# Expert bias on TensorE, D times x on ScalarE, gated output weights on VectorE, and a new order of work in an adaLN + Mamba-2 + MoE block

## What is computed

```python
mod = (silu(c) @ wmod)                      # sa, ca, ga, sb, cb, gb of each sequence
h = layernorm(x) * (1 + ca) + sa
x = x + ga * mamba2(h)                      # |ga| at least 0.25
h = layernorm(x) * (1 + cb) + sb
x = x + gb * moe(h)                         # |gb| at least 0.25
```

## Time and profile before

| | |
|---|---|
| median of 3 runs | 949.03 us (946.83 to 950.27) |
| the profiled execution | 949.21 us, of which the span from first to last instruction is 947.4 us |
| PE matmul busy | 701.8 us (74%) |
| DVE busy | 631.7 us (67%) |
| POOL busy | 596.0 us (63%) |
| ACT busy | 419.7 us (44%) |
| DMA | 93.05 MB, mean 98 GB/s |
| granted TensorE clock, mean | 0.871 |

### The profile page before, as it was taken

One profiled execution on the slowest core, in us unless ns is written; L12 is line 12 of the kernel. 1 busy time (PEld: TensorE's weight loads), 2 busy tenths in 40 slices (PEclk: granted clock), 3 DMA queues, 4 the chain that ended last, 5 costly groups with the idle time before them and its releaser, 6 DMA issues. The chain is left out here.

```text
span 947.4 us, 13162 instructions
## 1 busy us (share of the span) xinstructions
PE 701.8 (74%) x3642; PEld 549.3 (58%) x3642; DVE 631.7 (67%) x1654; ACT 419.7 (44%) x821; POOL 596.0 (63%) x437
## 2 busy tenths in 40 slices
PE   1578698698788799789978989788946737576570
PEld 1236466466566677667856767577835526454450
DVE  2445958978988997997999999988734413223230
ACT  2364663673774575467556654553323112111210
POOL 1035436567675878787878887797786654444444
PEclk9988987998899997989999999888979668777876
DMA  5000001111223554455356346435566685555642
GB/s 168 0 0 1 1 23 29 45 51 52 81 89 105 129 127 100 113 117 144 74 120 143 102 89 150 118 88 102 146 172 137 162 201 129 128 106 130 125 110 22
DMA packets 80456, 93.05 MB, mean 98 GB/s; under 512 B 7344, under 2 KB 66880, under 8 KB 80384
## 3 DMA queue, kind: packets, MB, share of 16 engines
q1 hardware_dynamic: 53712, 65.58, 24.7%
q0 software_dynamic: 26672, 26.62, 16.0%
HBM read 59.24 MB, written 32.93 MB: 97 GB/s over the span
## 5 line engine op out<-in xcount | busy, mean ns | idle before, releaser
L428 POOL DMA_INDIRECT out<-ro,xs x142 | 226.5, 1595 | 152.8 <-DVE ro L1026 79.3
L415 POOL DMA_INDIRECT rows<-payload,pos x128 | 134.8, 1053 | 47.0 <-issue 33.3
L824 DVE SCALAR_TENSOR_TENSOR xbc<-T,table,xbc 128x1022 f32<-128x1022 f32 (+2 forms) x96 | 122.7, 1278 | 31.5 <-ACT xbc L577 26.7
L1180 PE MATMUL T<-h,win 128*128 128x512 f32 x128 | 82.3, 777 | 56.4 <-DVE xbc L824 45.2
L1026 DVE SCALAR_TENSOR_TENSOR ro<-osum,xs 128x128 f32<-128x128 f32 x142 | 78.4, 594 | 60.0 <-DMA out<-ro,xs 59.8
L1343 PE MATMUL FX<-wt,hid 128*128 128x128 f32 x568 | 95.2, 322 | 31.2 <-DVE hid L1009 12.4
L1343 PEld LDWEIGHTS FX<-wt,hid 128*128 128x128 f32 x568 | 90.2, 232 | 43.3 <-DVE hid L1009 24.1
L626 ACT ACTIVATE xt<-FX 128x256 f32<-128x256 f32 x71 | 27.1, 382 | 188.3 <-PE FX L1323 176.8
L1333 PE MATMUL FG<-xt,wt 128*128 128x256 f32 x284 | 91.5, 453 | 6.3 <-issue 3.6
L619 ACT ACTIVATE sg<-FG,wt 128x256 f32<-128x256 f32 x142 | 59.2, 470 | 79.5 <-PE FG L1333 72.8
L1017 DVE TENSOR_TENSOR osum<-FX,wt 128x256 f32<-128x256 f32 x71 | 29.9, 421 | 85.1 <-PE FX L1343 76.2
(11 more groups left out here) (173 smaller groups left out, 1489.0 us busy)
## 6 DMA issues: line engine op xcount, KB each, us to landing
wt<-in_wt SPq DMA_DIRECT2D x71, 450.0 KB
xs<-rows SPq DMA_DIRECT2D x71, 258.0 KB
x<-in_x SPq DMA_DIRECT2D x8, 512.0 KB, 3.9
out<-x SPq DMA_DIRECT2D x8, 512.0 KB
rows<-pad SPq DMA_DIRECT2D x9, 258.0 KB, 5.0
out<-ro,xs POOLq DMA_INDIRECT x142
rows<-payload,pos POOLq DMA_INDIRECT x128
gate_a<-gates SPq DMA_DIRECT2D x8, 128.0 KB
```

The lines of the kernel that those rows point to most:

```text
L415: pool.indirect_dma_start(d["rows"], bass.IndirectOffsetOnAxis(ap=pos[:, k, n:n + 1], axis=0), payload[:, n, :], None).then_inc(scattered, 16)
L428: pool.indirect_dma_start(d["out"], bass.IndirectOffsetOnAxis(ap=xs[:, t % XSR, c, PAY - 1:PAY].bitcast(U32), axis=0), ro[:, t % 2, c, :], ...
L824: last = nc.vector.scalar_tensor_tensor(out=xbc[:, t, :, k:L], in0=T[:, :, 0:L - k], scalar=w, in1=xbc[:, t, :, k:L], op0=ALU.mult, op1=AL ...
L1180: last = nc.tensor.matmul(T[:, k, :], win[:, o:o + P], h[:, k * L:(k + 1) * L], start=True, stop=True)
```

## The change

- `expert_sum` and `osum` are gone. PE adds b3 by one more matmul for each 128 rows (a row of ones times the row of b3), two for each tile. `expert_out` reads FX in PSUM directly, into one of three `ro` buffers instead of two; PE's next use of FX waits for `ro_ready` instead of `o_taken`, and a weight buffer is free after `expert_down`.
- The landing of output adds is counted on two semaphores, for even and odd tiles; `add_out(t)` still waits for tiles t - 2 and t - 1.
- `weight_by_d` moves from POOL to ACT, as four activations with a scale for each chunk (16 for a pair). `gated_wo` moves from POOL to DVE.
- The expert of a tile is worked out from its row number (regions of 18432 rows in place of 8448), so three DVE instructions of `list_tiles` fall away.
- The order on all engines is new. On SP, weights now follow the rows of a same or later tile, `store_x1(i)` stands ahead of rows 8i - 17 and weights 8i - 18 and 8i - 17, and weights 8i - 23 stand behind rows 8i - 22. On POOL, `weight_by_decay(i, 1)` opens the step, and the dt and decay weights of chunk 2 stand behind two scatters and `add_out` of tiles 8i - 27 and 8i - 26. On ACT, `decay_exp` 0 to 7 stand together with no SiLU between them, and `expert_silu(8i - 18)` comes behind them; `softplus_exp` and `second_tanh` follow each other with no SiLU between.

The diff, cut (the order of DVE, and most of that of ACT and PE, is left out):

```diff
-REGION = NTOK + TR
+FIRST = TR
+REGION = 18432
-DUMP = E * REGION
+DUMP = E * REGION + FIRST
-WR, XSR = 4, 5
+WR, XSR, RR = 4, 5, 3
...
-        ro = sb("ro", [P, 2, 2, D])
+        ro = sb("ro", [P, RR, 2, D])
...
+        def landed(eng, t):
+            if t >= 0:
+                eng.wait_ge(added[t % 2], 32 * (t // 2 + 1))
...
             def load_weights(t):
                 sp_.wait_ge(seq_ready, pair_of_tile(t) + 1)
-                wait(sp_, o_taken, t - WR + 1)
+                wait(sp_, o_psum, t - WR + 1)
...
-                wait(sp_, added, 32 * (t - XSR + 1))
+                landed(sp_, t - XSR)
...
             for i in range(-3, 12):
-                if is_tile(PT * i - 23):
-                    load_rows(PT * i - 23)
-                if is_tile(PT * i - 22):
-                    load_rows(PT * i - 22)
                 if is_tile(PT * i - 21):
                     load_rows(PT * i - 21)
+                if is_pair(i):
+                    load_gates(i)
+                if is_tile(PT * i - 22):
+                    load_weights(PT * i - 22)
+                if is_tile(PT * i - 21):
                     load_weights(PT * i - 21)
...
                 if is_tile(PT * i - 18):
-                    load_weights(PT * i - 18)
                     load_rows(PT * i - 18)
+                if is_pair(i):
+                    store_x1(i)
                 if is_tile(PT * i - 17):
                     load_rows(PT * i - 17)
+                if is_tile(PT * i - 18):
+                    load_weights(PT * i - 18)
+                if is_tile(PT * i - 17):
                     load_weights(PT * i - 17)
-                if is_pair(i + 1):
-                    load_gates(i + 1)
                 if is_tile(PT * i - 16):
+                    load_rows(PT * i - 16)
                     load_weights(PT * i - 16)
-                    load_rows(PT * i - 16)
-                if is_pair(i):
-                    store_x1(i)
+                if is_pair(i + 3):
+                    reload_x(i + 3)
+                if is_tile(PT * i - 15):
+                    load_rows(PT * i - 15)
+                if is_tile(PT * i - 14):
+                    load_rows(PT * i - 14)
                 if is_tile(PT * i - 15):
                     load_weights(PT * i - 15)
-                if is_pair(i + 3):
-                    reload_x(i + 3)
-                if is_tile(PT * i - 14):
-                    load_weights(PT * i - 14)
...
             def add_out(t):
-                pool.wait_ge(ro_ready, t + 1)
-                pool.wait_ge(added, 32 * t) if t > 0 else pool.wait_ge(dump_set, 32)
+                if t == 0:
+                    pool.wait_ge(dump_set, 32)
+                landed(pool, t - 2)
+                landed(pool, t - 1)
                 pool.wait_ge(x1_stored, 16 * (pair_of_tile(t) + 1))
                 pool.wait_ge(xs_in[t % XSR], 16 * (t // XSR + 1))
+                pool.wait_ge(ro_ready, t + 1)
...
             for i in range(-2, 13):
                 if is_pair(i):
-                    weight_by_d(i, 1)
                     weight_by_decay(i, 1)
                 if is_pair(i - 2):
                     scatter(i - 2, 6)
-                if is_pair(i):
-                    weight_by_dt(i, 2)
                 if is_tile(PT * i - 27):
                     add_out(PT * i - 27)
                 if is_pair(i - 2):
                     scatter(i - 2, 7)
-                if is_pair(i):
-                    weight_by_decay(i, 2)
                 if is_tile(PT * i - 26):
                     add_out(PT * i - 26)
                 if is_pair(i):
-                    weight_by_d(i, 2)
-                    weight_by_dt(i, 3)
+                    weight_by_dt(i, 2)
+                    weight_by_decay(i, 2)
...
+            def weight_by_d(p, c):
+                act.wait_ge(tok_ready, C * p + c + 1)
+                wait(act, y_ready, C * p + c - 1)
+                for hh in range(NH):
+                    e = slice(hh * HD, (hh + 1) * HD)
+                    last = nc.scalar.activation(xskip[:, c % 2, :, e], tok[:, c, :, e], ACT.Copy, scale=d_row[:, hh:hh + 1])
+                last.then_inc(xskip_ready, 1)
...
+            def gated_wo(p):
+                vec.wait_ge(gate_a_in[p % 2], 16 * (p // 2 + 1))
+                wait(vec, out_psum, p)
+                nc.vector.tensor_tensor(out=wo[:, :, :, :], in0=woutn[:, :, :].unsqueeze(1).to_broadcast([P, 2, 2, D]),
+                                        in1=gate_a[:, p % 2, :, :].unsqueeze(2).to_broadcast([P, 2, 2, D]),
+                                        op=ALU.mult).then_inc(wo_ready, 1)
...
-                link(nc.vector.tensor_tensor(out=mine[:, 0:n, :], in0=mine[:, 0:n, :],
-                                             in1=experts.unsqueeze(1).to_broadcast([P, n, E]), op=ALU.mult))
-                link(nc.vector.tensor_reduce(out=tile_sum[:, 0:n], in_=mine[:, 0:n, :], axis=AX.X, op=ALU.add))
-                link(nc.vector.tensor_tensor(out=seq_e[:, span], in0=seq_e[:, span], in1=tile_sum[:, 0:n], op=ALU.add))
...
-                nc.vector.tensor_copy(tile_e[:, span], seq_e[:, span])
+                nc.vector.tensor_scalar(tile_e[:, span], seq_row[:, span], 1.0 / REGION, E - 0.6, ALU.mult, ALU.min)
...
-            def expert_sum(t):
+            def expert_out(t):
                 vec.wait_ge(o_psum, t + 1)
-                wait(vec, ro_ready, t)
-                nc.vector.tensor_tensor(out=osum[:, :, :], in0=FX[:, TR:2 * TR].rearrange("p (c m) -> p c m", c=2),
-                                        in1=wt[:, t % WR, B3:].unsqueeze(1).to_broadcast([P, 2, D]),
-                                        op=ALU.add).then_inc(o_taken, 1)
-
-            def expert_out(t):
-                vec.wait_ge(o_taken, t + 1)
-                rows_in = xs[:, t % XSR, :, :]
-                wait(vec, added, 32 * (t - 1))
+                landed(vec, t - RR)
                 for c in range(2):
-                    last = nc.vector.scalar_tensor_tensor(out=ro[:, t % 2, c, :], in0=osum[:, c, :], scalar=rows_in[:, c, 2 * D:2 * D + 1],
-                                                          in1=rows_in[:, c, D:2 * D], op0=ALU.mult, op1=ALU.mult)
+                    last = nc.vector.scalar_tensor_tensor(out=ro[:, t % RR, c, :], in0=FX[:, TR + c * D:TR + (c + 1) * D],
+                                                          scalar=xs[:, t % XSR, c, 2 * D:2 * D + 1], in1=xs[:, t % XSR, c, D:2 * D],
+                                                          op0=ALU.mult, op1=ALU.mult)
                 last.then_inc(ro_ready, 1)
...
                 for c in range(2):
+                    nc.tensor.matmul(FX[:, TR + c * D:TR + (c + 1) * D], ones_r[0:1, :].bitcast(F32), wt[0:1, t % WR, B3:B3 + D],
+                                     start=True, stop=False)
                     for f in range(FT):
                         last = nc.tensor.matmul(FX[:, TR + c * D:TR + (c + 1) * D], hid[:, t % 2, f, c * P:(c + 1) * P],
-                                                wt[:, t % WR, DOWN + f * D:DOWN + (f + 1) * D], start=(f == 0), stop=(f == FT - 1))
+                                                wt[:, t % WR, DOWN + f * D:DOWN + (f + 1) * D], start=False, stop=(f == FT - 1))
                 last.then_inc(o_psum, 1)
-                back["FX"] = (o_taken, t + 1)
+                back["FX"] = (ro_ready, t + 1)
```

More of the change, by code:

```diff
@@ L378, in weight_by_dt @@
                                         op=ALU.mult).then_inc(xdt_ready, 1)
-            def weight_by_d(p, c):
-                wait(pool, tok_ready, C * p + c + 1)
-                wait(pool, y_ready, C * p + c - 1)
-                nc.gpsimd.tensor_tensor(out=xskip[:, c % 2, :, :], in0=tok[:, c, :, 0:DI],
-                                        in1=d_row.unsqueeze(1).to_broadcast([P, 2, DI]), op=ALU.mult).then_inc(xskip_ready, 1)
             def weight_by_decay(p, c):
@@ L454, in _ @@
                 if is_pair(i):
-                    gated_wo(i)
-                    weight_by_d(i, 3)
+                    weight_by_dt(i, 3)
+                if is_tile(PT * i - 24):
+                    add_out(PT * i - 24)
+                if is_pair(i + 1):
+                    masked_da(i + 1, 0)
+                    masked_da(i + 1, 1)
                 if is_pair(i - 1):
                     scatter(i - 1, 0)
-                if is_tile(PT * i - 24):
-                    add_out(PT * i - 24)
-                if is_pair(i - 1):
                     scatter(i - 1, 1)
@@ L467, in _ @@
                 if is_pair(i + 1):
[L468 to L469 removed]
+                    masked_da(i + 1, 2)
+                if is_pair(i - 1):
+                    scatter(i - 1, 3)
                 if is_tile(PT * i - 22):
@@ L654, in _ @@
                     second_tanh(i - 1)
-                if is_tile(PT * i - 24):
-                    expert_silu(PT * i - 24)
+                if is_tile(PT * i - 22):
+                    expert_input(PT * i - 22)
+                if is_pair(i):
```

(59 more changed lines are left out.)

306 lines of the change are left out of this document (121 added, 185 removed).

## The result

The changed kernel takes 962.15 us (median of 4 runs, 956.55 to 964.64) beside 947.93 for the kernel before (4 runs): ratio 1.0138, with an interval of 1.0102 to 1.0175. It is slower by 1.4%; 923 us and faster were forecast. The profiled execution took 956.55 us (span 954.7).

A forecast was written before the change was run, and what follows sets the result against it. VectorE was taken to bound the four full steps (90% busy), TensorE close behind, with order bounding the head and something serial the tail. 949.2 - 17 (steps) - 3 (head) - 3 (last pair) - 3 (tail) = 923 us; range 906 to 938.

The forecast's parts named there:

- The steps: Four steps running scan, projection and experts together: PE 316 us busy plus 16 idle, 332 us, 17 less; ends 324 and 364.
- VectorE no longer bounds: Four steps: DVE falls from 315 to about 270 us, 77%, with 32 us of it from `ro` read from PSUM.
- the list of wrong signs: Included blocked time turning up at L845, L889 or the new `gated_wo`, leaving DVE near 85% in the steps.
- PE's waits down to a third: Sign of being right: PE's waits for L824 (taps) and for FX fall to a third.
- D on ScalarE: D products on ACT: 16 activations of 128 elements a pair, 6.4 us a pair; bounds 4 and 8.
- The bias: PE in the four steps: 60 more matmuls, priced like today's by their columns, add 15 us; ends 0 and 17.6.
- rival 2: TensorE takes over at once: bias dear, steps 350 us and gain nothing, the rest gains 9, 940 us; chance 0.13.
- The head: Fewer table loads and an earlier decay weight save 3 us over three or four steps; ends 8 less, 6 more.
- The moves off POOL: `weight_by_d` takes 5.5 us a pair off POOL; the 6.7 us step-opening wait was counted in PE's idle time.
- Last pair and tail: 3 us less in the last pair's step (ends 6 less, 2 more), 3 less in the tail (10 less, 6 more).
- Rival 3: Weights queued behind row loads that wait for scatters reach PE late, 34.5 us over five steps, 958 us; chance 0.14.
- Rival 1: Bigger gain: steps take 324 us, head, last pair and tail give their good ends, 900 us; chance 0.15.

The follow-up runs named there:

- e8: Kernel before with all parts of the change in the old order, bias on 128 rows, expert number and landing count as before: 916.6 us, ratio 0.9641.
- e4: Kernel before with only the one-row bias on PE and `ro` from PSUM, three `ro` buffers, old order, no moves: 950.1 us beside 950.6, ratio 1.0007.
- e10: e8 with, on DVE alone, `softplus_rest` ahead of `rows` and `y_chunk(i, 1)` behind them: 946.8 us, ratio 0.9970.
- e13: Changed kernel with bias on 128 rows, DVE's `y_chunk(i, 1)` and `softplus_rest` in their old places, POOL's masks 0 and 1 behind three scatters: ratio 0.9855.
- e6: Changed kernel with bias on 128 rows, `y_chunk(i, 1)` ahead of `rows`, `softplus_rest` behind taps 1, POOL's masks 0 and 1 behind three scatters: ratio 1.0087.
- e9: e8 with SP and POOL in the changed kernel's order: 1009.4 us, ratio 1.0598.
- e7: e6 with POOL's order, masks 0 and 1 included, left as in the changed kernel: ratio 1.0331.
- e11: e10 with PE's `project_in` 1 behind `ranks` and `inter` 1 behind `new_state` 2, as in the changed kernel: ratio 1.0417.
- e14: Kernel before with only D times x moved to ScalarE and `gated_wo` to VectorE: 920.4 us, ratio 0.9719.

## Why the prediction was wrong

The steps came out by the forecast's own structure: 316 busy and 16 idle were taken for PE, 326.6 busy and 16.7 idle were measured. Point by point:

- *VectorE no longer bounds:* right. 275.8 us in the steps for the 270 taken; `ro` at most 352 ns, and relieved by the 32 us taken (50.2 to 18.1). Some blocking did turn up at the decay product, as the list of wrong signs had it: 50.0 us in all (L852) for 46.2 before, and 42.1 in e8.
- *PE's waits down to a third:* right for the taps (16.8 to 1.5), not for FX (9.6 to 9.4, now on `ro`); the sum of idle time was right.
- *D on ScalarE:* 40.6 us for 128, 5.1 a pair, for 6.4 taken (bounds 4 and 8). *`gated_wo`:* 5.5 us for 8, as taken.
- *The bias, the first step that failed:* 0.29 us each, 15 for the steps, upper end 17.6, "as its columns are the same". It adds 26 us to PE's busy time in the steps (300.8 to 326.6, at a mean clock of 0.94 and then 0.96); 30 tiles at 1.12 would be 34. The range rested on the nearest row in columns, while this trace had no row with fewer than 128 rows among full ones; that difference should have opened the upper end. It is the 11 us of the steps' miss, and with it rival 2 (PE takes over; steps 350, 940 in all) was nearer than the forecast. e4 says the same: there the relief of DVE is paid for by PE, and the sum is zero.
- *The head, the second step that failed:* 3 us less, ends 8 less and 6 more; measured 14.5 more, and 17.5 of the miss of 33.5. "Order alone can lose there" was said and not worked out: `softplus_rest` and `rows` ahead of `y_chunk(i, 1)`, and `masked_da` beside them, could be read from the diff and from the step's timeline. e10 puts the fault in and e13 takes it out; e6 shows that the place of `softplus_rest` counts and not that of `y_chunk(i, 1)` alone. TensorE's clock had no term at all: the 10 us that the last three steps of the head grew by are busy time at the lower clock, not idle time.
- *The moves off POOL, mis-sized the other way:* they were counted in PE's idle time and in the head's 3 us; alone they give 25 to 27 us, 15 to 18 of it in the steps and 7 in the head. The bias with `ro` from PSUM, on which most of the forecast gain stood, gives 9.8 on top.
- *Last pair and tail:* 6 less were taken, 1.3 came. In the tail PE is busy 34 us more (135.2 to 169.6) and the tail is no longer or shorter (237.0 and 236.7), as landings bound it; here the row form's price is covered. The add of a tile still starts when the landing before it is in:

```profile
909.13 1.55 POOL L425 DMA_INDIRECT out<-ro,xs  x1 [4.62 <-DMA out<-ro,xs]
...
915.62 1.55 POOL L425 DMA_INDIRECT out<-ro,xs  x1 [3.08 <-DMA out<-ro,xs]
```

- *Rival 3:* did not happen (PE's waits in the steps have no line that ended with `wt`; 2.1 us at the first product ended in "issue"), but its mechanism is real, as e9 shows. *Rival 1:* its 900 was too far, but the parts without the two faults reach 914 to 917.

What stays open: why the steps of e6, e7 and e11 grew by 18 to 48 us is not traced beyond the waits and the clock; whether a drain is what the part form costs; which pauses of TensorE bring its clock down, and by how much each; which part of the rest of the new order makes e13 slower than e8 is not known either.

## What to carry to other kernels

Give a bias matmul the same 128 rows as its neighbours (an identity times a broadcast row) instead of a row of ones: the full form costs less than the part form, each time by 0.39 us here. When work is moved off a crowded engine, try the move alone before a new order: here the two moves gave 25 to 27 us and the new order took 24 back. In an order written by hand, list for each item put ahead who waits for what stands behind it, and what runs on POOL at that time; 3.4 us in the wrong place cost 7 us a step. And read the granted clock behind a new pause of TensorE: here 10 us of the changed kernel's longer head, and 11 of 20 in e10, were busy time at a lower mean clock, which no table of waits shows.

## What the runs showed of the hardware that I had not expected

- A matmul with 1, 32 or 64 rows of weights among ones with 128 rows holds TensorE for 0.41 us where one with 128 holds it for 0.22, and the four records behind it take 0.64 in place of 0.45. Between 1, 32 and 64 rows there is no difference.
- The load of one row of weights is no dearer than one of 128 (mean 200 and 209 ns, changed kernel), so nothing in the profile puts the price in the load:

```profile
L1335 PEld LDWEIGHTS FX<-wt,ones_r 1*128 1x128 f32 x284 | 45.6, 200 | 41.9 <-issue 26.9 <-DVE hid L1020 7.7
L1338 PEld LDWEIGHTS FX<-wt,hid 128*128 128x128 f32 x568 | 82.4, 209 | 19.1 <-issue 4.3
```

- Blocking by POOL moves on to the DVE instruction with two inputs in SBUF that stands beside it: 4.47 us for an addition of 0.69 (e10), 1.55 for `row_of`, which takes 0.29 alone. `wtop`, with one input, took 1.43 us beside `masked_da` (changed kernel, 247.48) and 0.17 alone (e14).
- A late operand can cost TensorE more than the wait for it: behind the wait that ended at 249.86 the granted clock is 0.50 for 9.14 us of work in the changed kernel.
